# A graph-attention kernel whose GpSimd pause after each gather is an iota of 256 columns in place of 64

## What is computed

```python
q = (feat @ Wq.T + bq).reshape(n, H, HD)          # n = 6250, H = 8, HD = 32
k = (feat @ Wk.T + bk).reshape(n, H, HD)
v = (feat @ Wv.T + bv).reshape(n, H, HD)
score = clip(einsum('ehd,ehd->eh', q[edge_dst], k[edge_src]) / sqrt(HD), -10, 10)
alpha = softmax of score over the edges of one destination
wv = segment_sum(alpha[:, :, None] * v[edge_src], edge_dst).reshape(n, C)
x = feat + wv @ Wp.T + bp
h = gelu(layernorm(x) @ W1.T + b1) @ W2.T + b2
out = layernorm(feat + x + h)
```

## Time and profile before

| | |
|---|---|
| median of 3 runs | 1149.14 us (1146.2 to 1150.38) |
| span of the profiled execution, first to last instruction | 1484.0 us |
| what the profiled execution took outside its span | not recorded |
| busy in the span: PE, DVE, ACT, POOL | 1135.0, 954.9, 672.3, 912.0 us |
| mean granted TensorE clock | 0.837 |
| DMA bytes | 312.25 MB, 154,887 packets |

### The profile page before, as it was taken

The page is one execution under the profiler, slowest core; times in us unless marked ns, Lnnn a source line. Parts: engine busy times, 40 slices in busy tenths (PEclk is TensorE's granted clock), DMA queues, the critical chain, the costliest instruction groups (busy, mean ns, idle before and its releaser), DMA issues.

```text
span 1484.0 us, 26187 instructions
## 1 busy us (share of the span) xinstructions
PE 1135.0 (76%) x6188; PEld 724.7 (49%) x6188; DVE 954.9 (64%) x1539; ACT 672.3 (45%) x1936; POOL 912.0 (61%) x1550
## 2 busy tenths in 40 slices
PE   8956778776977778777866876768877967877887
PEld 6823335454544454444544544544544544544566
DVE  6806676677676576666666666657667657666573
ACT  3212235455544545535544544535544535544543
POOL 4584667677776566766667566666667566666500
PEclk9976668999898788888798788887897788878699
DMA  9985877768777667776677676676677676676510
GB/s 328 314 253 178 254 227 225 229 199 253 214 220 225 203 188 222 227 232 196 197 237 208 191 230 197 199 236 179 206 236 209 191 238 196 197 225 199 180 54 23
DMA packets 154887, 312.25 MB, mean 210 GB/s; under 512 B 32200, under 2 KB 73126, under 8 KB 154791
## 3 DMA queue, kind: packets, MB, share of 16 engines
q0 software_dynamic: 61536, 200.85, 45.6%
q1 hardware_dynamic: 93254, 110.43, 23.3%
HBM read 270.02 MB, written 41.16 MB: 210 GB/s over the span
## 4 chain that ended last, share of the span: by engine, by line
PE 42%; another core or an unknown queue 23%; ACT 14%; issue 14%; DVE 5%; ACTq 1%; DVEq 0%; DMA 0%; SPq 0%
PE bank L483 9%; PE bank L503 7%; PE bank L951 5%; PE quad L875 4%; PE bank L930 3%; PE quad L942 3%; PE bank L977 3%; PE bank L964 2%; ACT hid L496 2%; PE bank L455 2%; ACT hid L491 1%; DVE kv L1636 1%; ACT hn L1276 1%; ACT staged L1217 1%
## 5 line engine op out<-in xcount | busy, mean ns | idle before, releaser
L401 POOL DMA_INDIRECT kv<-kv_rows,src_sb x750 | 721.5, 962 | 443.4 <-PE bank L951 212.1
L1616 DVE TENSOR_TENSOR prod<-kv,quad 128x1024 f32<-128x1024 f32 x196 | 239.3, 1221 | 346.6 <-remote 228.0
L1636 DVE TENSOR_TENSOR kv<-kv,bank 128x1024 f32<-128x1024 f32 x196 | 238.2, 1215 | 16.7 <-ACT kv L1209 16.7
L1623 DVE TENSOR_REDUCE score<-prod 128x32 f32<-128x1024 f32 x196 | 237.7, 1213 | 0.8
L483 PE MATMUL bank<-hT,w_sb 128*128 128x256 f32 x736 | 212.4, 440 | 17.9 <-ACT hid L491 17.9
L951 PE MATMUL bank<-kv,onehot 128*32 128x264 f32 x1568 | 150.1, 442 | 83.2 <-issue 49.5
L503 PE MATMUL bank<-w_sb,hid 128*128 128x256 f32 x736 | 205.3, 435 | 0.9 <-issue 0.7
L483 PEld LDWEIGHTS bank<-hT,w_sb 128*128 128x128 f32 x736 | 159.6, 222 | 52.5 <-issue 11.6
L942 PE MATMUL quad<-qwin,onehotT 32*128 32x256 f32 x1568 | 108.8, 354 | 95.7 <-issue 54.1
L503 PEld LDWEIGHTS bank<-w_sb,hid 128*128 128x128 f32 x736 | 159.8, 223 | 34.5 <-issue 8.7
L930 PE MATMUL bank<-staged,place 128*128 128x264 f32 x196 | 81.5, 502 | 113.8 <-ACT staged L1217 76.0
(11 more groups left out here) (164 smaller groups left out, 1421.0 us busy)
## 6 DMA issues: line engine op xcount, KB each, us to landing
qwin<-q_rows SPq DMA_DIRECT2D x392, 64.0 KB
dst_rows<-edge_dstT SPq DMA_DIRECT2D x50, 256.0 KB
q_rows<-q_next SPq DMA_DIRECT2D x25, 512.0 KB
kv_rows<-kv_out SPq DMA_DIRECT2D x24, 512.0 KB
kv<-kv_rows,src_sb POOLq DMA_INDIRECT x750
agg_rows<-acc_sb SPq DMA_DIRECT2D x98, 82.5 KB
xT_sb<-xT SPq DMA_DIRECT2D x25, 256.0 KB, 5.4
xq_sb<-xT SPq DMA_DIRECT2D x25, 256.0 KB
```

Source lines behind the costliest of these rows:

```text
L401: return nc.gpsimd.indirect_dma_start(out=rows, out_offset=None, in_=kv_dram, in_offset=bass.IndirectOffsetOnAxis(ap=index, axis=0))
L1616: nc.vector.tensor_tensor(prod[:, slot % 2].rearrange("p (i c) -> p i c", c=C), kv[:, slot, :, 0:C], quad[:, :, 0:C], ALU.mult).then_inc(s ...
L1623: nc.vector.tensor_reduce(score[:, slot % 2], prod[:, slot % 2].rearrange("p (h d) -> p h d", d=HD), AX.X, ALU.add).then_inc(s_score, 1)
L1636: nc.vector.tensor_tensor(kv[:, slot, :, C:2 * C].rearrange("p i (h d) -> p i h d", d=HD), kv[:, slot, :, C:2 * C].rearrange("p i (h d) -> ...
```

## The change

One constant is changed. `PAUSE` stands in two places: the size of `idle_rows` (line 162: 128 partitions, 2 x 4 x `PAUSE` floats, so 2 KB a partition before and 8 KB now) and the length of the iota (line 830). The number and the order of instructions are the same on every engine; of the 750 iotas each writes 128x256 in place of 128x64. Waits and semaphores are the same.

```diff
@@ -15,7 +15,7 @@
 HALF_TURN = SLOTS // 2
 HALF = 16
 WIN = 32
-PAUSE = 64
+PAUSE = 256
 WINDOW_STARTS = (0, 10, 25, 41)
```

## The result

The kernel after takes 1272.06 us (median of 4, 1271.34 to 1272.5) against 1149.46 us: a ratio of 1.107, 95% interval 1.104 to 1.109. It is slower by 123 us. The forecast was 1260, in a range of 1185 to 1290.

What follows compares the result with a forecast made beforehand. The prediction took GpSimd's issue of gathers to bound the timed runs: 1149 us, plus 115 us for 750 longer iotas, less 4 us hidden in the wait at the start, gives 1260 us, range 1185 to 1290.

Steps and rivals of the forecast that it cites:

- That GpSimd binds: Timed runs are bound by GpSimd's issue of gathers, DMA second; with the iota near 358 ns, 1260 us, chance 68%.
- GpSimd's clockwork: GpSimd repeats gather, iota, gap as 0.96 + 0.21 + 0.16 us; 79.6 + 995 + 60.8 us gives 1136.
- The page's rule: DMA-bound needs the issuing engine's track solid with DMA slices; by it GpSimd has room and the change costs nothing, 1149 us.
- The price of the iota: Line 830 on GpSimd: 205 ns grows to 358 at 0.80 ns a column, plus 153 ns, 750 times 115 us.
- Gather and gap: On GpSimd, gathers stay 0.96 us and the gap behind the iota 0.16 us, in series with it; cadence 1.48 us.
- The fill at the start: GpSimd's first 27 gathers precede a 17.51 us wait for `sums`; their longer iotas, 4 us, are hidden in it.
- The 13 us left over: Between GpSimd's 1136 us and the median 1149, 13 us remain for all of GpSimd's waiting in a timed run.
- SP slowed by recording: Recording delays SP's register moves and `qwin` issues, holding DVE and ACT; the profiled execution thereby loses 335 us.
- The profiled span stays near 1484: GpSimd's idle time before gathers absorbs the 115 us in the profile: span within 2% of 1484 us, at most 1515.
- No change: Rival: the longer pause hides in GpSimd's idle time, needing an old cadence of 1.19 us; 1149 us, chance 9%.
- partly hidden: Rival: GpSimd's timed cadence lies between 1.19 and 1.31 us, hiding some added time; 1160 to 1230 us, chance 12%.
- Faster, by pacing: Rival: wider-spaced gathers let `qwin` loads land sooner on the DMA engines, shortening DVE's waits; 1138 us, chance 5%.

Runs made afterwards that it cites:

- e1: The kernel before, recorded once more without any edit, on a chip where it takes 1148 to 1149 us: median 1148.23 us, recorded execution 1146.12 us.
- e2: The kernel before with the iota cut from 64 columns to 1 (PAUSE = 1): 1112.24 us, ratio 0.969.
- e4: The kernel before with the iota lengthened from 64 columns to 128 (PAUSE = 128): 1194.69 us, ratio 1.042.
- e11: The kernel before (64 columns) with one more reduce over 256 numbers a batch on DVE: 1153.3 us, ratio 1.0045.
- e10: The kernel after with one iota of 1024 columns behind each batch's last gather, replacing 256 columns behind every gather: 1260.72 us, ratio 1.098 to the kernel before.
- e12: The kernel before without the iotas and the wait on their semaphore, with one more DVE reduce a batch: 1144.42 us.

## Why the prediction was right, and where it was not

**That GpSimd binds.** Right, against the page it was read from. The sum of 1136 us from GpSimd's clockwork and the timed median of 1149 carried it, and e1, e2, e4 and e11 show it. The page's rule (the Trainium skill, "Perfetto Trace Analysis", What "DMA-bound" means) isn't fulfilled even in the good recording: the gathers fill 63% of e1's span, gathers and iotas 88% of the time from the first gather to the last iota, and what lies between is the 0.16 us after each iota. The measurement decides here: what shows the bound is that GpSimd next to never waits and that its added time comes out whole.

**The price of the iota.** 153 ns were forecast, 161 measured (365 - 204). The slope was 0.84 ns a column, the memsets', and not the 0.80 of the short iotas. That is 6 of the 12 us by which the time was missed.

**Gather and gap.** "Still 0.16" was nearly right. The idle time before the gathers grew by 4.6 us, 6 ns each, and the gathers by 1.4. That is the other 6 us.

**The fill at the start.** Wrong. Of GpSimd's wait of 17.51 us the runs on common chips have nothing: in e1 and in the kernel after no wait for `sums` of that size exists, since the first product starts at 95 us and not at 115.7. The 4 us that the longer iotas were to swallow there were never idle. With the 12 above this makes 16; the medians differ by 122.6 us where the recorded executions differ by 126.0, and so 12 are left.

**The 13 us left over.** They weren't waits. In e1, 6.3 us lie between GpSimd's last iota and the last product, 1.8 around the span (1146.1 against 1144.3), and from the first gather to the last iota it is 997.5 us where 995 were reckoned; the recorded execution was 2 us under the median. The head and the tail of the sum (79.6 and 60.8 us) held, with 79.5 and 61.0 in e1, though they were read from the other kind of recording.

**SP slowed by recording.** Wrong, in cause and in place. e1 has a span of 1144.3 us with a recording, and on the late chip the kernel before takes 1494 us as the median of 19 executions. It goes with the chip, or with its state at that time, and what DVE and ACT were held by in the earlier trace rows is TensorE's late semaphore increments. The forecast was saved because it took the timed median, and not the span, as its base.

**The profiled span stays near 1484.** Wrong for the same reason: 1270.3.

**The rivals.** No change and partly hidden are out by e2 and e4. "Faster, by pacing" is wrong on a common chip: down to a cadence of 1.25 us every shorter pause was faster. On the late chip two kernels with about as much GpSimd time as the kernel after were 6 to 7% faster than before. The kernel after itself was not run there, so whether this very change turns its sign is open, and so is why increments come late and why a longer pause helps; that fewer gathers in flight let them through is only argued.

## What to carry to other kernels

Before a wait in a trace is explained, hold the span against the timed median: where they differ by 29%, as here, the recording may be of a machine that the timed runs never saw, and only durations in undisturbed stretches carry over. An engine with a constant cadence can be checked against the median by a plain sum, head + count x cadence + tail; when that comes to the median within about 1%, it is at the bound or next to it, whatever its busy share says. Whether another engine stands just behind, the sum doesn't tell; a run with a shorter filler, or with more work on the other engine, does. And where that engine binds, lengthening a filler instruction on it is paid in full, once for each time it runs, while taking it out gives back less, since the gap that it hid comes back. An experiment that adds an instruction to load an engine should be read from that engine's stream and not from the instruction's duration: here nearly half of the load was something else.

## What was not expected of the hardware

- A gather straight behind a gather starts 0.30 us after its end, behind an iota 0.16 us after the iota's. Removing an iota of 0.204 us gains 0.074 us a gather (1.325 to 1.251), not 0.36.
- DVE's clip (line 1630, in e10 line 1631) is sometimes held up by GpSimd. Its means are 200 ns without an iota, 196, 223, 214 and 293 with 1, 64, 128 and 256 columns, and 385 with one of 1024 a batch. It isn't the length of the iota alone: the longest clip in e1 (416 ns) and in the kernel after (692) ran beside a gather, began 0.54 and 0.26 us into it and ended within 12 ns of its end, and the longest in e10 (1640) ran beside a gather and the iota of 1003 ns behind it, and ended 0.04 us after that. The Trainium skill, "SBUF — State Buffer", Who interferes with whom, says that `tensor_scalar` can hold a port pair that DVE shares with GpSimd, and that the later one waits for the whole instruction; the ends of these three agree, while a median clip beside a gather in e1 took 200 ns and was hardly held. It costs DVE 14 us here, beside a wait that is longer.
- Two runs with one more small DVE instruction a batch (e11, e12) have a standstill of some 4 us in DVE's stream once a loop round that the kernels without it don't have.
- On one chip TensorE's semaphore increments came up to several us late and SP's register moves took up to 0.9 us, with the same program, and the time was 30% longer.
